# The back part's batch of rows fetched by four gathers on GpSimd's queue instead of one plain transfer on SyncE's

## The reference, cut to what matters

```
xn = _layernorm(x, ln_scale, ln_bias)
scores = jnp.einsum('bhid,bhjd->bhij', q, k)
probs = jax.nn.softmax(scores / jnp.sqrt(jnp.float32(HIDDEN_DIM)), axis=-1)
out = jnp.einsum('bhij,bhjd->bhid', probs, v) ; out = ... + xn
```

## Time and profile before

| | us |
|---|---|
| median of 3 runs | 2253.99 (2253.25 to 2261.86) |
| the profiled execution's own time | 2249.78 |
| its span, first to last instruction | 2248.0 |
| front part ends, back part begins | about 1291 to 1293 |
| last store issued | 2245.48 |

### The profile page before, as it was taken

The page is one execution under the profiler, slowest core; times in us unless marked ns, Lnnn a source line. Parts: engine busy times, 40 slices in busy tenths (PEclk is TensorE's granted clock), DMA queues, the critical chain, the costliest instruction groups (busy, mean ns, idle before and its releaser), DMA issues. The chain is left out here.

```text
span 2248.0 us, 34225 instructions
## 1 busy us (share of the span) xinstructions
PE 1996.7 (89%) x12660; PEld 1369.6 (61%) x12660; DVE 1687.3 (75%) x4160; ACT 1083.7 (48%) x1907; POOL 585.0 (26%) x621
## 2 busy tenths in 40 slices
PE   3998989898999899889989758999999999999997
PEld 3787778777877787777877623444444444444443
DVE  5767776767766776767677449888888888888882
ACT  3333323333333333333333117777777777777774
POOL 2331332223222323233313031222222222222211
PEclk9999999999999999999999959999999999999999
DMA  3000000000000000000000032222222222222220
GB/s 117 6 10 10 1 10 10 10 1 10 10 10 5 6 10 10 10 1 10 10 6 1 10 98 71 76 76 76 76 75 76 76 76 76 76 76 79 70 69 10
DMA packets 47941, 85.28 MB, mean 38 GB/s; under 512 B 5728, under 2 KB 9056, under 8 KB 47712
## 3 DMA queue, kind: packets, MB, share of 16 engines
q1 hardware_dynamic: 45872, 81.32, 11.4%
q10 hardware_dynamic: 1904, 1.78, 0.2%
HBM read 49.26 MB, written 34.87 MB: 37 GB/s over the span
## 5 line engine op out<-in xcount | busy, mean ns | idle before, releaser
L1263 DVE TENSOR_REDUCE b_nm<-b_MX 128x1 f32<-128x512 f32 x1024 | 647.6, 682 | 74.1 <-PE b_MX L1379 66.8
L1163 ACT ACTIVATE b_pr<-b_ST 128x512 f32<-128x512 f32 x1024 | 550.8, 601 | 163.1 <-PE b_ST L1366 161.9
L1379 PE MATMUL b_MX<-b_kt,b_qt 32*128 32x512 f32 x1024 | 353.9, 511 | 43.0 <-DMA b_qt<-staging 10.1
L383 ACT ACTIVATE s<-G 128x512 f32<-128x512 f32 x306 | 182.9, 598 | 432.7 <-PE G L685 423.7
L690 PE MATMUL Y<-w_wd,h 128*128 128x128 f32 x2448 | 335.3, 281 | 8.6 <-DVE h L544 7.9
L690 PEld LDWEIGHTS Y<-w_wd,h 128*128 128x128 f32 x2448 | 315.4, 195 | 24.0 <-DVE h L544 13.3
L535 DVE TENSOR_TENSOR su<-U,s 128x512 f32<-128x512 f32 x272 | 186.1, 684 | 161.3 <-ACT s L383 83.3
L1366 PEld LDWEIGHTS b_ST<-b_qm,b_kt 32*128 32x128 f32 x1024 | 119.1, 185 | 304.6 <-ACT b_pr L1163 190.8
L1366 PE MATMUL b_ST<-b_qm,b_kt 32*128 32x512 f32 x1024 | 293.6, 503 | 10.8 <-ACT b_pr L1163 10.7
L1394 PE MATMUL b_PV<-b_pr,b_va 128*32 128x512 f32 x2048 | 280.5, 620 | 0.0
L544 DVE TENSOR_TENSOR h<-C,su 128x512 f32<-128x512 f32 x272 | 188.1, 691 | 9.3
(11 more groups left out here) (237 smaller groups left out, 3497.3 us busy)
## 6 DMA issues: line engine op xcount, KB each, us to landing
b_kt<-staging SPq DMA_DIRECT2D x64, 256.0 KB, 2.9
b_qt<-staging SPq DMA_DIRECT2D x64, 256.0 KB, 3.4
staging<-b_khi SPq DMA_DIRECT2D x32, 256.0 KB, 3.0
staging<-b_qhi SPq DMA_DIRECT2D x32, 256.0 KB, 3.0
xin<-in_x SPq DMA_DIRECT2D x17, 256.0 KB, 2.6
mid<-xo SPq DMA_DIRECT2D x17, 256.0 KB, 2.0
b_x<-mid SPq DMA_DIRECT2D x16, 256.0 KB, 2.9
staging<-b_klo SPq DMA_DIRECT2D x16, 256.0 KB, 3.0
```

What stands on the lines that cost most here:

```text
L383: nc.scalar.activation(sbuf_s[n % 2][:], G[n % 2][:], ACT.Silu).then_inc(act_done.sem, 1)
L1163: nc.scalar.activation(pr[k % 2][:, j], bank[:].rearrange("p a b -> p (a b)"), ACT.Exp, scale=SM_SCALE).then_inc(used["st"].sem, 1)
L1263: nc.vector.tensor_reduce(nm[g % 2][:, t, c:c + 1], bank[:].rearrange("p a b -> p (a b)"), AX.X, ALU.max).then_inc(used["mx"].sem, 1)
L1379: pe.matmul(flat(MX[place % MX_BANKS]), qt[g][rows_of(j), u // HG % T], flat(kt_[g])[rows_of(j)], start=True, stop=True).then_inc(made["mx ...
```

## The change: what it does

A host array `c_rows` holds the numbers 0 to 511 as 128 x 4 unsigned integers (partition p has 4p to 4p+3), and goes to the SBUF tile `rows` by one small transfer on SP, in the place of the load of batch 0. Where SP loaded a batch with one transfer, GpSimd now issues four indirect transfers, one for each t: each takes for every partition p the row number `rows[p, t]` and fetches that row, 512 bytes, of the batch's slot in `mid`. The same bytes come to the same places. The four gathers of batch 0 stand behind the memsets and a wait for `rows`; those of batch B+2 stand at the end of GpSimd's iteration B, behind `xfb` and behind the same wait for `xx` of batch B. VectorE waits for 64 instead of 16 on the semaphore `loaded`. In the front part SP copies 2 batches (512 KB) from `x` to the first two slots of `mid`, DRAM to DRAM, and waits for that before `load(0, -1, 2)`.

```diff
@@ front, SP
+            sp.dma_start(mid_dram[0:PAD], x_dram[0:PAD]).then_inc(padded, 16)
+            sp.wait_ge(padded, 16)
             load(0, -1, 2)
@@ back
-        loaded = [sig(f"loaded{p}", 16) for p in range(2)]
+        loaded = [sig(f"loaded{p}", 16 * T) for p in range(2)]
@@ back, SP
             def batch_steps(B):
-                nxt, prv, ahead = B + 1, B + -1, B + 2
-                if ahead.exists:
-                    if B.exists:
-                        sp.wait_ge(xx_ready.sem, B.at(xx_ready, 1))
-                    p = ahead.parity
-                    sp.dma_start(x[p][:], md[ahead.number + PAD]).then_inc(loaded[p].sem, 16)
+                nxt, prv = B + 1, B + -1
                 fetch(B, 3)
...
-            sp.dma_start(x[0][:], md[PAD]).then_inc(loaded[0].sem, 16)
+            sp.dma_start(rows[:], rows_dram).then_inc(rows_loaded, 16)
@@ back, GpSimd
+            def gather(B):
+                p = B.parity
+                for t in range(T):
+                    nc.gpsimd.indirect_dma_start(
+                        x[p][:, t], None, mid_dram.rearrange("b n d -> (b n) d"),
+                        bass.IndirectOffsetOnAxis(ap=rows[:, t:t + 1], axis=0),
+                        element_offset=(B.number + PAD) * N * D).then_inc(loaded[p].sem, 16)
...
                     nc.gpsimd.tensor_tensor(xfb[:], xf[:], w["b2h"][:], ALU.add).then_inc(xfb_ready.sem, 1)
+                if ahead.exists:
+                    if B.exists:
+                        pool.wait_ge(xx_ready.sem, B.at(xx_ready, 1))
+                    gather(ahead)
...
             own.settle()
+            pool.wait_ge(rows_loaded, 16)
+            gather(Batch(0, 0))
             program(batch_steps)
@@ back, VectorE
-                    dve.wait_ge(loaded[p].sem, nxt.at_own(loaded[p], 16))
+                    dve.wait_ge(loaded[p].sem, nxt.at_own(loaded[p], 16 * T))
```

More of the change, by code:

```diff
@@ L243, in build_front @@
         oT_ready = sig("oT_ready", N_ATT)
+        padded = ctx.enter_context(nc.semaphore("padded"))
         comb_cleared = ctx.enter_context(nc.semaphore("comb_cleared"))
@@ L876, with build_back @@
 MX_PLACE = {one: _p for _p, one in enumerate(MX_RING)}
-def build_back(nc, weights, mid_dram, out_dram, staged_dram, tail_dram, batches):
+def build_back(nc, weights, mid_dram, out_dram, staged_dram, tail_dram, rows_dram, batches):
     w = weights
@@ L939, in build_back @@
         fetched = [sig(f"fetched{g}", 32) for g in range(GRP)]
+        rows = ctx.enter_context(nc.sbuf_tensor("b_rows", [P, T], mybir.dt.uint32))
+        rows_loaded = ctx.enter_context(nc.semaphore("b_rows_loaded"))
         preset = ctx.enter_context(nc.semaphore("b_preset"))
@@ L1087, in rsqrt @@
                 nc.gpsimd.tensor_tensor(rs[:, :, 0], ve[:], w["minus_half"][:], ALU.pow).then_inc(rs_ready[k].sem, 1)
+            def gather(B):
[5 more added lines that the diff above has]
+                        element_offset=(B.number + PAD) * N * D).then_inc(loaded[p].sem, 16)
             def batch_steps(B):
-                nxt, prv = B + 1, B + -1
+                nxt, prv, ahead = B + 1, B + -1, B + 2
                 if nxt.exists:
@@ L1641, in lay_out @@
         "c_tail": tail,
+        "c_rows": np.arange(N, dtype=np.uint32).reshape(P, T),
     }
@@ L1663 @@
             build_front(nc, w, args["x"], mid, args["c_ident"], NB // 2)
-        build_back(nc, w, mid, out, staging, args["c_tail"], NB)
+        build_back(nc, w, mid, out, staging, args["c_tail"], args["c_rows"], NB)
     r = run_bass_kernel_spmd(nc, [arrays], core_ids=[0])
```

## The result

| | before | changed |
|---|---|---|
| median | 2253.31 us (18 runs, 2247.06 to 2264.79) | 2264.19 us (18 runs, 2261.61 to 2273.36) |
| ratio | | 1.0045, 95% interval 1.0031 to 1.0059 |
| profiled execution: time, span, mean granted clock | 2249.78, 2248.0, 0.970 | 2264.51, 2262.7, 0.965 |

The kernel became slower by about 10 us: 2253.31 x 0.0045 = 10.1, with an interval of 7.0 to 13.3 (the medians stand 10.9 apart). The forecast was +9.6 and 2263.6. The two profiled executions stand 14.7 us apart, more than the medians, and the first task is to divide these 14.7 us.

The account below looks back on a forecast made before the run. TensorE is busy 89% of the span, and only the back part's start, waiting for batch 0, was taken as exposed. 8.9 for the start plus 0.7 contention gave +9.6 us on 2253.99, so 2263.6; range 2256 to 2271.

Parts of the forecast that it names:

- signs of being wrong: `b_ve` before 1302 or after 1311, a steady iteration longer by over 0.3 us, or the front part's end moving.
- The place: Start of the back part, batch 0: the one load without cover, so anything added there is added to the time.
- The size of the start: Back part's start: four gathers of 1.27 us behind the memsets plus 2.3 us landing make `b_ve` 8.9 us later.
- Contention with the staging: Back part's start: up to three of batch 1's gathers (192 KB) run beside the staging transfers, +0.7 us.
- The iterations: Later batches: gathers have 39.7 us of cover against 7.4 needed, so they were counted as 0.
- The front copy: Front part: SP's 512 KB DRAM copy has 43.8 us of cover, counted as 0; 1.9 us if it pressed on the first load.
- The bound of the comparison: Whole kernel: about 0.5%, 11.3 us, can be told from no change, 2242.7 to 2265.3; same 0.53, slower 0.44, faster 0.03.
- Dear gathers: Rival at the exposed start: a gather holds GpSimd over 1.7 us, making the kernel slower by over 0.5%; chance 0.28.
- Cheap gathers: Rival at the exposed start: gathers cost SP's issue time of 0.32 us, so +5.1 us and 2259.1; chance 0.10.
- One-off: Rival at the first gather: a first-use cost like ScalarE's 1.28 us table load, +10.9 and 2264.9; chance 0.07.

Follow-up runs that it names:

- e2: Changed kernel, but batch 0 alone comes by SP's plain transfer, batches 1 to 15 by gathers; ratio 1.0008 to the kernel before.
- e9: Changed kernel with four plain transfers on GpSimd's queue in place of the four gathers, no row numbers read; ratio 1.0025 to the kernel before.
- e1: Kernel before with only the front part's 512 KB DRAM copy and SP's wait added; ratio 1.0026 to the kernel before.
- e8: Changed kernel with 22 memsets ahead of each iteration's gathers, delaying them about 41 us; 2383.51 us, ratio 1.0561 to the kernel before.
- e10: Changed kernel with batches 0 and 1 by SP's plain transfers, batches 2 to 15 by gathers; one run, 2265.43 us.
- e11: Kernel before, unchanged, timed against itself and profiled a second time; ratio 0.9976.
- e7: Changed kernel with 15 memsets ahead of each iteration's gathers, delaying them about 28 us; ratio 1.0043 to the kernel before.
- e5: Changed kernel with one gather per batch, batch 0's ahead of the memsets, constant rows issued only once batch 0 is there; one run, span 2250.8 us.
- e3: Changed kernel with one gather per batch of 128 rows of 2 KB instead of four of 512-byte rows; ratio 1.0043 to the kernel before.

## Why the prediction was right

**In short.** The path was right and its price nearly so: all that is shown of the change's own cost lies in the exposed start of the back part. That the median came within 0.6 us of 2263.6 is in part luck. The profiled execution was forecast at 2257.6 us of span and took 2262.7, since its front part ended 5.67 us later, by the clock; and the 4.2 us by which the medians were taken to lie above the profiled execution, from three runs, are -0.3 us in the changed kernel (2264.19 against 2264.51). The two misses cancel.

**Its own signs of being wrong.** Two of the three came: `b_ve` is at 1311.65, behind 1311, and the front part's end moved. Neither speaks against the mechanism, for both are absolute times: the back part of the unchanged program began at 1293.28 in one profile and at 1290.23 in the other, and counted from there `b_ve` was forecast at 4.12 + 8.9 = 13.0 us and came at 12.70. The signs were badly chosen, since they do not allow for a front part that shifts. The third, a steady iteration longer by over 0.3 us, did not come (780.84 us for fourteen instead of 780.35).

**The place.** The exposed start alone pays: shown by e2 (batch 0 plain, start back to 4.17 and 1.0008) and by the unchanged length of the iterations.

**The size of the start.** Predicted +8.9, measured +8.58. The four gathers were taken at 5.1 us, from a full-size add of 1.27 each; they take 4.94, since each is 0.95 with a gap of 0.30 in front (the first 1.18). Two small terms were off and nearly cancelled: the first gather starts 0.63 us behind the last memset's end and not 0.1, and the landing behind the end of the last issue, taken as 2.3, is 1310.27 - 1308.56 = 1.7. The statistics took 1.38 instead of 1.46. That the add had the size of a gather was luck: no row tied the one to the other, and e9 shows that a plain DMA there is 0.59.

**Contention with the staging, +0.7.** Not shown: e1, e8, e10 and e11 put the 0.48 us seen inside the scatter of that stretch, and leave room for some 0.3. The term was bounded at 0.7 and then taken in full without a row that asked for it.

**The iterations, 0.** Right, and e7 and e8 bracket the point at which the cover ends, as computed (32.6 us of delay by e8, 32.7 by the rows).

**The front copy, 0.** Right within what can be told; four copies cost nothing.

**The bound of the comparison.** The text called 11.3 us what a measurement can tell, and gave 0.53 to a time inside it, hardly more than to a time beyond it. The measured +10.1 is inside, and its interval of 1.0031 to 1.0059 is clear of 1, but e11 shows that such an interval is too narrow by itself. That this one is nevertheless a real loss rests on the 8.58 us of the timelines, which e7 and e8 repeat at 12.58 and 12.70 of start.

**The rivals.** Dear gathers: refuted, 1.25 us is below the 1.7 from which it decides. Cheap gathers: refuted, e9's plain transfers come nearest. One-off: the first gather is dearer by 0.23 us, and by 0.3 of gap, not by 1.28 or more, and e5 refutes a cost of microseconds. The Trainium skill, "GPSIMD Engine Reference", section 2.1, gives about 6 us for the first call of a freshly loaded kernel; no run here shows such a time at the first gather. The Trainium skill, "DMA: Bandwidth & Descriptors", section "Anatomy of one DMA — SWDGE (gpsimd) path", has about 2.0 us fixed per DMA plus the bytes at 436 GB/s. The data of the changed kernel's last gather arrive 2.57 us after its start, 0.4 more than the 2.15 us estimated from that page. The four overlap: from the first one's start to the last landing it is 6.6 us, not the 8.6 that the prediction estimated from that page for four in turn.

**What stays open.** Why some executions keep TensorE at 1.2 GHz at the end of the front or lose 3 us in the second iteration, and whether the change makes that likelier: the slow front end stands in the profiles of the changed kernel and of e10 and in none of the other gather kernels, the long second iteration in those of e3 and e10. The end of the back part adds a third such place (e10). The 1.5 us between 8.6 and the measured 10.1 are not explained further, and lie within the scatter. But the clock may well have a share in them: all 18 runs of the changed kernel had a mean granted clock of 0.967 or less, 16 of them 0.965 or less, while 42 of the 88 runs of the kernel before that were timed beside the experiments, on four chips, had 0.969 or more. The 9 us of longer start, if all at half clock, would take only 0.002 off the mean (9 x 0.5 / 2262, an estimate). The fastest runs stand 14.6 us apart (2261.61 and 2247.06), as the two profiles do. That the slow front end stands in most runs of the changed kernel would fit this; only the one was profiled, so it is not shown.

## What to carry to other kernels

A transfer moved to another engine's queue costs nothing where its data have tens of microseconds of cover, even at over ten times the issue time (4.94 us against 0.43), and its full issue time plus landing where a pipeline fills. So look first for the one batch without cover, and leave that one on the fast queue (e2). When a difference is under half a per cent, measure the stretch in the profile rather than the whole, time the old kernel against itself once, and profile it a second time: only some stretches repeat. State a sign of being wrong as a length from an event of the same stretch, not as an absolute time.

## What the runs showed of the hardware that was not expected

- A gather of 128 rows of 512 bytes holds GpSimd 0.95 us, with 0.30 us in front of the next; the first of four takes 1.04 us, and the program's first 1.18. 128 rows of 2 KB take no longer (1.04, and 1.18 the first). Four plain DMAs on the same queue took 2.37 us.
- A gather that shares the DMA engines with 1 MB of other transfers, issued 1.5 us ahead of it, lands after 6.1 us instead of 3.5.
- Two timings of one program, 12 runs against 23, differed by 0.24% with an interval of 0.10 to 0.39%. In two profiles of it one stretch repeated to 0.01 us (4.12 and 4.13), and another, 131.0 us long in the one, took 136.9 in the other, with the granted clock at 0.75 where it had been 1.00.
